# A graph network's edge loop: where the first edge layer is computed, and how many row buffers it has

## The reference

```python
# layer 0, experts
h1 = relu(einsum('bsd,edh->bseh', features, expert_w1) + expert_b1)
h2 = relu(einsum('bseh,ehf->bsef', h1, expert_w2) + expert_b2)
expert_out = einsum('bseh,eho->bseo', h2, expert_w3) + expert_b3
# layer 1, edge convolution; edge_length_embedded is [edges, 8], fc_w0 [8, 64], fc_w1 [64, 256]
hid = silu(edge_length_embedded @ fc_w0 / sqrt(8))
w = hid @ fc_w1 / sqrt(64)
# products of the four parts of w with h[edge_src] and edge_attr, then
y = segment_sum(products, edge_dst)
```

## Time and profile before

| | us |
|---|---|
| runs | 3951.26, 3951.65, 3953.61 |
| median | 3951.65 |
| span of the profiled execution | 3966.1 |
| expert phase | 2157 to 2507 |
| edge loop, units | 2647 to 3354 |

### The profile page before, as it was taken

One profiled execution on the slowest core, in us unless ns is written; L12 is line 12 of the kernel. 1 busy time (PEld: TensorE's weight loads), 2 busy tenths in 40 slices (PEclk: granted clock), 3 DMA queues, 4 the chain that ended last, 5 costly groups with the idle time before them and its releaser, 6 DMA issues. The chain is left out here.

```text
span 3966.1 us, 60201 instructions
## 1 busy us (share of the span) xinstructions
PE 3642.8 (92%) x18935; PEld 3087.8 (78%) x18935; DVE 2451.9 (62%) x4843; ACT 1491.9 (38%) x3475; POOL 665.9 (17%) x658
## 2 busy tenths in 40 slices
PE   5999899999999999999996999988888888869996
PEld 2555699999999998999994888657777777848885
DVE  7886655555555555556554666556666665677775
ACT  0363311211211111112114544457777775136663
POOL 0002000000000000000002200025555553012221
PEclk9999999999999999999997999989999999879998
DMA  1353022222222222222222210112222222431113
GB/s 53 65 105 65 26 87 89 65 89 84 70 84 74 80 88 71 83 83 71 83 69 98 72 31 30 42 47 83 81 84 79 84 80 59 150 71 38 38 38 119
DMA packets 265216, 288.48 MB, mean 73 GB/s; under 512 B 70331, under 2 KB 237327, under 8 KB 264283
## 3 DMA queue, kind: packets, MB, share of 16 engines
q1 hardware_dynamic: 233701, 208.44, 18.1%
q0 software_dynamic: 24192, 66.15, 5.8%
q10 hardware_dynamic: 7030, 10.16, 0.7%
HBM read 242.21 MB, written 42.48 MB: 72 GB/s over the span
## 5 line engine op out<-in xcount | busy, mean ns | idle before, releaser
L1043 PE MATMUL bank<-a_wide,parts 125*128 125x448 f32 x4200 | 872.9, 367 | 0.0
L1043 PEld LDWEIGHTS bank<-a_wide,parts 125*128 125x128 f32 x4200 | 785.6, 188 | 78.4 <-issue 9.9
L2288 POOL DMA_INDIRECT rows<-h_dram,src_t x392 | 375.4, 958 | 331.9 <-DVE prod L2483 218.7
L2421 ACT ACTIVATE hot<-eq,ea 128x80 f32<-128x80 f32 x1568 | 405.3, 352 | 1.0 <-DVE eq L2463 0.5
L1093 DVE CAST a_wide<-a_cols 125x2240 fp32r<-125x2240 bf16 x210 | 275.5, 1328 | 138.7 <-PE bank L1043 138.7
L1017 POOL TENSOR_TENSOR nf_g<-nf,nf_g 128x896 fp32r<-128x896 f32 x42 | 95.4, 2271 | 1575.0 <-ACT nf_g L1187 1575.0
L2328 PEld LDWEIGHTS bank<-prod,hot 128*80 128x80 f32 x2352 | 295.9, 153 | 70.9 <-issue 21.6
L2328 PE MATMUL bank<-prod,hot 128*80 128x128 f32 x2352 | 331.8, 277 | 10.6 <-issue 10.4
L1052 PE MATMUL bank<-nf_g,whh 128*128 128x448 f32 x1512 | 339.7, 369 | 0.0
L1052 PE MATMUL bank<-msg,wc 128*128 128x448 f32 x1512 | 339.1, 369 | 0.0
L1052 PEld LDWEIGHTS bank<-msg,wc 128*128 128x128 f32 x1512 | 284.2, 188 | 27.5
(11 more groups left out here) (438 smaller groups left out, 5787.7 us busy)
## 6 DMA issues: line engine op xcount, KB each, us to landing
a_cols<-a_dram SPq DMA_DIRECT2D x210, 546.9 KB
a_dram<-a_cols SPq DMA_DIRECT2D x15, 1250.0 KB, 9.9
w<-in_w SPq DMA_DIRECT2D x4, 2728.0 KB
deg_bc<-deg_dram SPq DMA_DIRECT2D x42, 224.0 KB, 6.0
gate_bc<-gate_dram SPq DMA_DIRECT2D x42, 224.0 KB, 3.2
rows<-h_dram,src_t POOLq DMA_INDIRECT x392
w<-y_rows SPq DMA_DIRECT2D x12, 512.0 KB, 15.1
w<-in_w SPq DMA_DIRECT2D x6, 896.0 KB
```

The costliest lines, as they stand in the source:

```text
L1043: ins = nc.tensor.matmul(p_msg[f][:, 0:GW], parts[0:SPB, m, c * HB + k, f * 128:(f + 1) * 128], a_wide[u % 2][0:SPB, k, :], start=(c == 0 ...
L2288: nc.gpsimd.indirect_dma_start(out=rows[n % ITC][:, :], out_offset=None, in_=h_dram, in_offset=bass.IndirectOffsetOnAxis(ap=src_t[:, n:n + ...
L2421: ins = nc.scalar.activation(hot[:, q % 2, j, m, :], eq[:, q % 2, j, :], ACT.Copy, scale=ea4[:, q * UC + j, m:m + 1])
```

## The change

The hidden layer of the edges leaves the loop. `expert_mlp` computes it in 98 pieces of 256 columns, three in each step from i = 5 on, and stores both parts in `hid_dram`. The 8 weights' rows are padded to a 128 x 128 matrix with two diagonal blocks, so that one piece covers half a pair of units: rows 0 to 63 belong to the even unit and rows 64 to 127 to the odd one. A piece is one matmul into bank 7, two activations that read it (the rounded part, and the float32 value), a subtraction on GpSimd, and a store of 128 x 2 x 256 from one of three result buffers. SP loads three blocks of 16 rows for a piece, three pieces ahead. The piece places on TensorE are after layer 1, after layer 2 and at the step's end. `turn` moves from the start of a step to behind its layer 3, and for the tiles before the last group it has bank 6 alone. In the loop, SP loads for each unit two blocks of 64 x 512 into one of 7 buffers, and there are 14 row buffers instead of 8. The high rows are stored once rather than twice, fw0's preparation and three memories' clearing in `norm_and_galerkin` go, and a register in the adjacency phase is clamped at zero.

```diff
+ROWS_AHEAD = 14
+HIDS = 7
+HE = 256
+PIECES = 2 * NIT
+FIRST_STEP = 5
...
-                for at_row, part, ready in ((0, 0, ea_high), (16, 0, ea_high), (8, 1, ea_low)):
+                for at_row, part, ready in ((0, 0, ea_high), (8, 1, ea_low)):
...
 def expert_mlp
+                def edges(n):
+                    if n < PIECES:
+                        i, h = divmod(n, 2)
+                        units = ea8_dram.rearrange("(m a) (i u c) -> m i u a c", m=PARTS, i=NIT, u=2)[:, i, :, :, h * HE:(h + 1) * HE]
+                        sp.dma_start(ea[n % 3][0:16, :].bitcast(F32), units[0]).then_inc(ea_in[n % 3], 16)
+                        sp.dma_start(ea[n % 3][16:32, :].bitcast(F32), units[1]).then_inc(ea_in[n % 3], 16)
+                        sp.dma_start(ea[n % 3][32:48, :].bitcast(F32), units[0]).then_inc(ea_in[n % 3], 16)
+                def move(n):
+                    i, h = divmod(n, 2)
+                    sp.wait_ge(hid_mm, START + n + 1)
+                    edges(n + 3)
+                    sp.wait_ge(hid_low, START + n + 1)
+                    sp.dma_start(hid_dram[i, :, :, h * HE:(h + 1) * HE].rearrange("m p e -> p m e"), hid[:, n % 3, :, :].bitcast(F32))\
+                      .then_inc(hid_out[n % 3], 16)
...
+                for n in range(PIECES):
+                    pool.wait_ge(silu_done, START + n + 1)
+                    nc.gpsimd.tensor_tensor(hid[:, n % 3, 1, :], hid[:, n % 3, 1, :].bitcast(F32), hid[:, n % 3, 0, :], ALU.subtract)\
+                      .then_inc(hid_low, 1)
...
+                def edge_layer(n):
+                    pe.wait_ge(fw_step, START + 3)
+                    pe.wait_ge(gate_done, START + 1)
+                    pe.wait_ge(ea_in[n % 3], START + n // 3 * 48 + 48)
+                    pe.wait_ge(silu_done, START + n)
+                    nc.tensor.matmul(p_hid[:, 0:HE], fw[:, :], ea[n % 3][:, :], start=True, stop=True).then_inc(hid_mm, 1)
+
                 def turn(t):
-                    pe.wait_ge(added, START + t - 1)
+                    if t < SOON:
+                        pe.wait_ge(added, START + t)
...
                 for i in range(NI + 2):
-                    for t in turns(i):
-                        pe.wait_ge(y_out, START + (i - 1) // E0 * KD)
-                        turn(t)
                     if i + 1 < NI:
                         layer1(i + 1)
+                    for n in piece(i, 0):
+                        edge_layer(n)
                     if i < NI:
                         layer2(i)
+                    for n in piece(i, 1):
+                        edge_layer(n)
                     if 0 < i <= NI:
                         layer3(i - 1)
+                    for t in turns(i):
+                        pe.wait_ge(y_out, START + (i - 1) // E0 * KD)
+                        turn(t)
+                    for n in piece(i, 2):
+                        edge_layer(n)
...
+                    act.wait_ge(hid_mm, START + n + 1)
+                    act.wait_ge(hid_out[n % 3], START + n // 3 * 16)
+                    for m in range(PARTS):
+                        to = hid[:, n % 3, m, :]
+                        ins = nc.scalar.activation(to if m == 0 else to.bitcast(F32), p_hid[:, 0:HE], ACT.Silu,
+                                                   scale=8.0 ** -0.5)
+                    ins.then_inc(silu_done, 1)
...
 def edge_convolution
-        rows = [sb(ctx, f"rows{j}", [EC, D]) for j in range(ITC)]
+        rows = [sb(ctx, f"rows{j}", [EC, D]) for j in range(ROWS_AHEAD)]
...
-                        sp.wait_ge(hid_mm, units + q - 1)
-                        sp.dma_start(ea8[0:24, b, :].bitcast(F32), ea8_dram[:, q * UE:(q + 1) * UE]).then_inc(ea_in[b], 16)
+                        sp.wait_ge(w_mm, chunks + max(q - HIDS + 1, 0) * UC)
+                        for m in range(PARTS):
+                            sp.dma_start(hid[m * MUL:(m + 1) * MUL, q % HIDS, :].bitcast(F32),
+                                         hid_dram[pair, m, u * MUL:(u + 1) * MUL, :]).then_inc(hid_in[q % HIDS], 16)
...
-                        pool.wait_ge(p_done, chunks + n + 1 - ITC)
+                        pool.wait_ge(p_done, chunks + n + 1 - ROWS_AHEAD)
...
-                            pe.wait_ge(hid_done, units + q + 1)
+                            pe.wait_ge(hid_in[q % HIDS], loads + q // HIDS * 32 + 32)
```

More of the change, by code:

```diff
@@ L1716, in expert_mlp, with piece, turned_in @@
         gate_p = [h2[m][0:NT, 1, :, :].rearrange("p k n -> p (k n)")[:, 0:E0 * RT].rearrange("p (e n) -> p e n", n=RT) for m in range(PARTS)]
-        p_h1, p_h2, p_y, p_x = bank[0:2], bank[2:4], bank[4:6], bank[6:8]
+        p_h1, p_h2, p_y, p_x, p_hid = bank[0:2], bank[2:4], bank[4:6], bank[6:8], bank[7]
+        def piece(i, spot):
+            n = 3 * (i - FIRST_STEP) + spot
+            return range(n, n + 1) if 0 <= n < PIECES else range(0)
+        def turned_in(t):
+            return p_x[0] if t < SOON else p_x[t % 2]
         def ready_tiles(g):
@@ L1759, in _ @@
                     gate_load(i)
+                sp.dma_start(fw_raw[:, :], A["fw0"]).then_inc(fw_in, 16)
+                sp.wait_ge(ea_zero, START + 3)
+                for n in range(3):
+                    edges(n)
                 for m in range(8, NM):
                     weights(m)
-                for i in range(4, NI):
-                    gate_load(i)
+                for i in range(4, NI + 4):
+                    for n in piece(i - 4, 0):
+                        move(n)
+                    if i < NI:
+                        gate_load(i)
+                    for spot in (1, 2):
+                        for n in piece(i - 4, spot):
+                            move(n)
                     if i == WKV_AT:
@@ L2353, in _ @@
                     next_round(pe, regs, per_round)
-                units, chunks, dmas = at_round(pe, regs, per_round)
+                units, chunks, loads = at_round(pe, regs, per_round)
                 pe.wait_ge(added, units)
```

176 lines of the change are left out of this document (84 added, 92 removed).

## The result

The changed kernel takes 3979.23 us (3974.42 to 3982.0, 4 runs) against 3951.8 us of the kernel before in the same comparison: a ratio of 1.0067, with an interval of 1.0055 to 1.008. It is 27 us slower. The forecast was 3942, the range ended at 3972, and the likeliest case had the wrong sign.

The account below looks back on a forecast made before the run. TensorE was taken as nearly full in the expert phase, a ring of waits as bounding the edge loop. +15.6 - 5 - 22.5 + 2 = -9.9 us from 3951.65 gave 3942, range 3850 to 3972.

Parts of the forecast that it names:

- Expert phase: Expert phase: added matmuls +20.1, moved turn -6.5, activations' wait +2, together +15.6 us (bounds +2 and +42).
- The moved turn: Expert phase, TensorE: a third layer before the turn removes most waits for ScalarE's output, -6.5 us (bounds -7.9 and 0).
- the activation's tight wait: Expert phase: the middle piece's matmul may wait for the first piece's two activations, 0 to +10 us, taken as 2.
- Loop, start: Edge loop's start: first weights need only a load, so first sums come earlier, -5 us (bounds -7 and -2).
- Loop, middle: Middle of the edge loop: TensorE sheds 98 hidden matmuls of 0.23 us, -22.5 us (from nothing to at most 121).
- rival 3: Edge loop does not move, its ring being trains of gathers and landings: +10.6 us, 3962; chance 0.12.
- The +2 for heavier loads: Middle of the edge loop: 20.4 MB more loads cost some of the gain, +2 us.
- Row buffers: Edge loop: 14 row buffers instead of 8 add no gain in the likeliest case, since stalls count from the train's end.
- the gathers' landing or late signals: Edge loop's stalls: something other than the matmul's recorded end holds the waits; named as where the prediction could be most wrong.
- Rival 1: Edge loop: the row buffers were the ring, so 14 make the loop TensorE's, -91 us there, 3871; chance 0.27.
- Rival 2: Edge loop: new loads delay gathers' landing, lengthening 86 stalls by 0.5 us each, +31 us in sum, 3983; chance 0.16.
- Rival 4: Edge loop: VectorE's casts hold up the gathers' descriptors, so removing them gains 42 us more, 3900; chance 0.05.

Follow-up runs that it names:

- 8 buffers: The changed kernel with 8 row buffers instead of 14: 3966.96 us against 3952.66 of before, ratio 1.0034.
- plain row loads: The changed kernel with GpSimd's gathers replaced by SP's plain loads of 128 neighbouring rows: 3832.72 us, ratio 0.9658 to before.
- trains of six: The kernel before with clamp, moved turn, 14 row buffers and gathers in trains of exactly 6: ratio 0.9981 on the 3843 us chip, 1.0109 on one with stalls.
- plain loads from GpSimd: The changed kernel with GpSimd's indirect gathers replaced by its own plain transfers of 128 neighbouring rows: 3831.31 us, ratio 0.969 to before.
- The unread gathers: The changed kernel with all used rows loaded by SP, while GpSimd issues 392 gathers into buffers nobody reads: 3998.92 us, ratio 1.008 to before.
- 14 buffers at 1.0018: The kernel before with the clamp and 14 row buffers instead of 8, nothing else: 3975.9 us, ratio 1.0018.

## Why the prediction was wrong, point by point

**Expert phase: right.** +15.6 said, +18 measured (12 to 25 by the interval), +14.4 in the trace. Inside it a piece was dearer in my sum than it is: +14.4, with TensorE's waits that I counted down from 9.6 to 8.0 us, leaves (14.4 + 1.6) / 98 = 0.16 us a piece, not 0.205; my lower bound by columns should have read 0.204 x 256 / 448 = 0.12, not 0.10. The moved turn gave some 7 for my 6.5, the activation's tight wait came once (1.2 us, I took 2), and the 3.1 us for loads I had not seen. The clamp is 0 as said.

**Loop, start: right.** -5 said, -4.6 in the trace.

**Loop, middle: wrong, and this is the step that failed.** "So I take for the likeliest only what TensorE sheds, 98 x 0.23 = -22.5 us, for the stretches between stalls." Measured: +0.6 us with everything in, some 5 less than before with 8 buffers in traces that differ by more than that from chip to chip, and by medians nothing. The step took TensorE's path as the loop's path between stalls. But a stall ends with GpSimd's train, a product's weights having been ready 4.1 us before, and the next train starts from that restart; what TensorE sheds turns into waiting. Part of it is lost in another way, which my sum had no term for: the lower granted clock, some 70 us of the loop at 1.2 GHz instead of 40. What that costs the loop is open: with 8 buffers the clock is 0.95 too and the loop 8.5 us shorter. I had the ring and its lower bound of 0 as rival 3, and gave it 0.12; no row spoke for the value that I took. The +2 for heavier loads has no support either: with plain row loads at a share of 0.49 they delay nothing. The term has its size where TensorE does bound the loop: first sums to last add are 571.4 us with the hidden layer (trains of six, on the chip without stalls) and 548.4 without it (plain loads from GpSimd), 23 us less, across two chips and two ways of loading. By that the change would be worth -23 - 4.6 + 18, some 10 us, where there are no stalls. It did not run on that chip, so this is an estimate; the nearest run there, the changed kernel with plain row loads and unread gathers of 16 rows, took 17.6 us less than before (3825.57 against 3843.15).

**Row buffers: wrong.** I had them at nothing, with 0.27 for a large gain; they cost 8 us or more. I had named "the gathers' landing or late signals" and left it there. The unread gathers rule out the first; the second fits all runs, but since TensorE stops now and then where it waits for nobody, late signals are not the whole of it.

**Rival 1** fell with 14 buffers at 1.0018. **Rival 2**, slower by the transfers, had the sign but not the cause: with plain row loads beside the same new loads, at a share of 0.49, nothing stalls. So the rule of the Trainium skill, "DMA: Bandwidth & Descriptors", section "Queues, rings and completion order", on signals behind other writes, has no visible price here; a product of that run starts 0.04 us after its weights. **Rival 3** came nearest, 3962 by it; it lacks the buffers' 8 to 13 us. **Rival 4**, the casts, fell too: the unread gathers' kernel has no casts and stalls all the same, so what the Trainium skill, "SBUF — State Buffer", section "SBUF: two separate sides", says of copies that lock GpSimd out is not the cause of these stalls.

**What stays open:** by what an indirect gather close behind another holds the others up (TensorE's signals on their way out, the others' receipt of them, or the engines themselves); why it was not seen on one chip; what the lower clock costs; half of the buffers' price.

## What to carry to other kernels

When engines that wait for different counts of one engine restart at the same instant, look for what they restart after, before costing anything; in before that was the last gather's end, with 80% of the restarts between 0.95 and 1.38 us behind it (52 of 65). In this loop, whose bound wasn't named, work taken off an engine that was idle 12% of the time counted as zero, and where it went it counted in full (18 us in a phase that was full). And a buffer that lets a disturbing engine run further ahead can cost time. When a wait looks late, count which matmul it really needs before measuring the lateness: here it was 4.1 us, not the 1.5 that the nearest one suggests.

## What the runs showed of the hardware that I had not expected

- In all comparisons but one, a train of indirect gathers from GpSimd, 1.25 us apart, is followed by a restart of the waiting engines 1.1 to 1.7 us after its last gather (medians). In before that is 4.1 us after the end of the weights that VectorE waits for. It is so whether the rows are read or unread, scattered or neighbouring, 128 or 16. Plain transfers of 128 KB from the same engine don't do it, nor do gathers 2.8 us apart.
- The same program takes 3843 us on one chip and 3952 to 3969 on the others, and the loop has the difference: 571 us from first sums to last add in a version of before there, 694 to 703 in before's loop elsewhere.
- The granted clock of a loop with stalls is 0.95 to 0.98 here, and 1.00 in the loops without them.
- With all rows by plain loads the loop runs at 5.6 us a unit (548 us), TensorE never idle. The indirect gathers cost some 150 us here, over five times what the change moved.
